# The last attention head of a fused attention and feed-forward kernel, worked through by token tiles in four passes

## What is computed

```python
x = L0_attn_x                                   # (2, 2048, 512) float32
x = x + attention(layernorm(x), Wq, Wk, Wv, memory, memory_norm, memory_weight)
x = x + ffn(layernorm(x), weight, weight_scale, input_scale)

# attention: 4 queries x 8 heads of 16 features; keys and values have 8 heads
scores = einsum('bsqhd,bthd->bqhst', qh, kh) * scale
a_dot  = einsum('bqhst,bthd->bsqhd', softmax(scores), vh)
a_mem  = sigma_q @ memory / (sigma_q @ memory_norm)          # sigma_q = elu(q)
out    = a_dot * (1 - w) + a_mem * w
# ffn
x_fp8 = clip(x / input_scale, -448, 448).astype(float8_e4m3fn)
y     = (x_fp8 * input_scale) @ (weight * weight_scale).T
```

## Time and profile before

| | |
|---|---|
| median of 3 runs | 2065.68 us (2064.96 to 2067.22) |
| the profiled execution's own time | 2065.7 us |
| its span in the profile | 2064.0 us |
| PE busy | 2029.0 us (98%), 27379 instructions |
| ACT busy | 1933.2 us (94%) |
| DVE busy | 1118.2 us (54%) |
| POOL busy | 82.3 us (4%) |
| first exponential of the heads starts | 211.6 us |
| last exponential of the heads starts | 2038.3 us |

### The profile page before, as it was taken

One profiled execution on the slowest core, in us unless ns is written; L12 is line 12 of the kernel. 1 busy time (PEld: TensorE's weight loads), 2 busy tenths in 40 slices (PEclk: granted clock), 3 DMA queues, 4 the chain that ended last, 5 costly groups with the idle time before them and its releaser, 6 DMA issues.

```text
span 2064.0 us, 62714 instructions
## 1 busy us (share of the span) xinstructions
PE 2029.0 (98%) x27379; PEld 897.5 (43%) x27380; DVE 1118.2 (54%) x1716; ACT 1933.2 (94%) x2180; POOL 82.3 (4%) x135
## 2 busy tenths in 40 slices
PE   8999999999999999999999999999999999999996
PEld 4555443334444444444444444444444444444442
DVE  5775544555445555455554555545555445555456
ACT  4555999999999999999999999999999999999995
POOL 3322000000000000000000000000000000000000
PEclk9999999999999999999999999999999999999998
DMA  5656211111111211112121111221121211121111
GB/s 191 196 186 206 62 48 35 36 48 51 51 42 39 72 50 51 40 44 61 50 51 50 53 49 51 51 65 36 45 49 51 71 37 43 51 71 51 33 43 42
DMA packets 137558, 131.57 MB, mean 64 GB/s; under 512 B 31520, under 2 KB 113824, under 8 KB 137312
## 3 DMA queue, kind: packets, MB, share of 16 engines
q1 hardware_dynamic: 135248, 125.11, 21.8%
q10 hardware_dynamic: 2064, 2.69, 0.4%
HBM read 86.57 MB, written 37.49 MB: 60 GB/s over the span
## 4 chain that ended last, share of the span: by engine, by line
PE 97%; DVE 2%; ACT 1%; DMA 0%; issue 0%; ACTq 0%; POOL 0%; DVEq 0%; POOLq 0%
PE ps L753 43%; PE ps L775 43%; PE ps L698 6%; PE ps L810 1%; PE ps L796 1%; PE ps L713 1%; PE ps L667 1%; DMA mem_aug<-in_memory_norm 0%; ACT pool L641 0%; DVE ps L1018 0%; DVE pool L906 0%; DVE parts L931 0%; DVE work L1177 0%; PE ps L682 0%; PE ps L675 0%
## 5 line engine op out<-in xcount | busy, mean ns | idle before, releaser
L641 ACT ACTIVATE pool<-ps 128x1024 f32<-128x1024 f32 x1984 | 1823.8, 1152 | 8.8 <-PE ps L753 5.7
L753 PE MATMUL ps<-q_st,k_st 99*32 99x512 bf16 x16384 | 1121.2, 379 | 3.2 <-issue 3.2
L775 PE MATMUL ps<-pool,v_st 128*32 128x512 f32 (+1 forms) x8704 | 1080.0, 567 | 0.5 <-ACT pool L641 0.5
L753 PEld LDWEIGHTS ps<-q_st,k_st 99*32 99x32 bf16 x16384 | 459.7, 96 | 815.7 <-issue 500.6
L775 PEld LDWEIGHTS ps<-pool,v_st 128*32 128x32 f32 x8704 | 281.5, 110 | 206.7 <-ACT pool L641 1.4
L1102 DVE STREAM_TRANSPOSE by_token<-ps 128x512 f32<-128x512 f32 x64 | 45.9, 717 | 484.0 <-PE ps L775 484.0
L1095 DVE SCALAR_TENSOR_TENSOR parts<-parts 128x1024 f32<-128x1024 f32 x192 | 235.3, 1225 | 6.6
L1081 DVE TENSOR_SCALAR parts<-ps 128x512 f32<-128x512 f32 x128 | 88.6, 692 | 131.4 <-PE ps L753 131.4
L698 PE MATMUL ps<-pool,wqT 128*128 128x512 f32 x256 | 111.4, 592 | 0.0
L596 ACT ACTIVATE parts<-ps 128x512 bf16<-128x512 f32 x40 | 23.9, 597 | 62.5 <-PE ps L698 62.5
L1154 DVE SCALAR_TENSOR_TENSOR y_out<-ps,scalars,resid 128x512 f32 x28 | 21.0, 752 | 113.2 <-PE ps L796 113.2
(11 more groups left out here) (125 smaller groups left out, 740.4 us busy)
## 6 DMA issues: line engine op xcount, KB each, us to landing
q_st<-q_aug SPq DMA_DIRECT2D x384, 64.0 KB
v_st<-v_aug SPq DMA_DIRECT2D x64, 256.0 KB
q_aug<-parts SPq DMA_DIRECT2D x96, 128.0 KB
k_st<-k_aug SPq DMA_DIRECT2D x64, 192.0 KB
sigma_kept<-y_out SPq DMA_DIRECT2D x32, 256.0 KB, 3.6
k_st<-k_aug SPq DMA_DIRECT2D x64, 128.0 KB
wqT<-sigma_kept SPq DMA_DIRECT2D x32, 256.0 KB, 3.3
resid<-in_x SPq DMA_DIRECT2D x7, 1024.0 KB, 9.1
```

Source lines behind the costliest of these rows:

```text
L641: act.activation(held[:, half_u * 2 * CH:half_u * 2 * CH + 2 * CH], sc[unit % SLOTS].rearrange("p a b -> p (a b)"), ACT.Exp, scale=EXP_UNIT)\
L753: last = pe.matmul(dst[VW * c:VW * c + VW, :], k_st[0:AUG, par, keys:keys + VW], q_st[0:AUG, par, q * CH:q * CH + CH], start=True, stop=True)
L775: last = pe.matmul(acc[par][VW * c:VW * c + VW, :].rearrange("v (i s) -> v i s", s=VW)[:, places, :], v_st[:, par, j, :], by_place[:, c, p ...
```

## The change

The last head is taken out of the loop over heads and worked through in four passes, one for each token tile. A pass has eight units (`TILE_UNITS`); a unit is now two key tiles x 4 queries x the 128 tokens of that tile, again 1024 columns. All 32 units of this head go to ACT; there is no late half and no `late_exps` on DVE. Products with the values follow three units behind (`last_weigh`), accumulate in `acc[1]` and `acc[0]` in turn, and have 128 columns in place of 512. After each pass DVE adds that tile's 128 tokens to the residual (`add_last_tile`), takes its statistics (`tile_moments`) and rounds it (`round_to_float8` into `xq[:, t]`). The last tile of chunk 6 gets its product at units 5 to 8 of this head, and its `ffn_out` stands ahead of the first pass's result. DVE's loop over chunks now ends at chunk 6, and chunk 7 is written out. At the end, the output of tile 0 is written between the statistics and the rounding of tile 3, and PE's order is turn 0, turn 1, product 0, turn 2, product 1, turn 3, product 2, product 3.

```diff
+LAST_HEAD = NG * HEADS - 1
+TILE_UNITS = ST // 2
+LAST_UNITS = TPC * TILE_UNITS
+LAST_RING = 2 * RING
+LAST_PRODUCT_AT = (5, 6, 7, 8)
...
         def _(act):
...
-            for n in range(NG * HEADS):
+            for n in range(LAST_HEAD):
...
+            for v in range(LAST_UNITS):
+                unit = LAST_HEAD * UNITS + v
+                act.wait_ge(scores_ready, unit + 1)
+                act.activation(last_probs[:, v % LAST_RING, :, :, :].rearrange("p x q s -> p (x q s)"),
+                               sc[unit % SLOTS].rearrange("p a b -> p (a b)"), ACT.Exp, scale=EXP_UNIT)\
+                    .then_inc(probs_ready, 1)
...
         def _(pe):
...
+            def last_scores(v):
+                unit = LAST_HEAD * UNITS + v
+                t, pair = divmod(v, TILE_UNITS)
+                by_tile = q_st[0:AUG, 1, :].rearrange("r (q t s) -> r t q s", q=QG, t=TPC)[:, t, :, :]
+                pe.wait_ge(probs_ready, unit - SLOTS + 1 + THREE_FREE)
+                for x in range(2):
+                    for c in range(P // VW):
+                        keys = (2 * pair + x) * P + c * VW
+                        last = pe.matmul(sc[unit % SLOTS][VW * c:VW * c + VW, x, :], k_st[0:AUG, 1, keys:keys + VW], by_tile,
+                                         start=True, stop=True)
+                last.then_inc(scores_ready, 1)
+
+            def last_weigh(v):
+                t, pair = divmod(v, TILE_UNITS)
+                by_place = last_probs[:, v % LAST_RING, :, :, :].rearrange("p x q (c s) -> p x c q s", c=P // VW)
...
+                for x in range(2):
+                    for c in range(P // VW):
+                        last = pe.matmul(acc[1 - t % 2][VW * c:VW * c + VW, 0:QG * VW].rearrange("v (q s) -> v q s", q=QG),
+                                         v_st[:, 1, 2 * pair + x, :], by_place[:, x, c, :, :],
+                                         start=(pair == 0 and x == 0), stop=(pair == TILE_UNITS - 1 and x == 1))
+                last.then_inc(pv_done, 1)
...
+            for v in range(LAST_UNITS):
+                last_scores(v)
+                if v + UNITS in WEIGH_AT:
+                    weigh_v(LAST_HEAD - 1, 0, WEIGH_AT[v + UNITS])
+                if v >= SLOTS:
+                    last_weigh(v - SLOTS)
+                if v in LAST_PRODUCT_AT:
+                    ffn_product((NG - 1) * TPC - 1, LAST_HEAD, LAST_PRODUCT_AT.index(v))
+            for v in range(LAST_UNITS - SLOTS, LAST_UNITS):
+                pe.wait_ge(probs_ready, LAST_HEAD * UNITS + v + 1 + THREE_FREE)
+                last_weigh(v)
...
-            for t in range(0, TPC, 2):
+            last_ffn_turn(0)
+            for t in range(1, TPC):
                 last_ffn_turn(t)
-                last_ffn_turn(t + 1)
-                last_ffn_product(t)
-                last_ffn_product(t + 1)
+                last_ffn_product(t - 1)
+            last_ffn_product(TPC - 1)
...
         def _(dve):
...
+            for t in range(TPC):
+                add_last_tile(t)
+                tile_moments(NT - TPC + t)
+                if t == TPC - 1:
+                    last_out(0)
+                round_to_float8(NT - TPC + t, xq[:, t, :], last_chunk=True)
+            for t in range(1, TPC):
+                last_out(t)
```

More of the change, by code:

```diff
@@ new lines, in _ @@
+            for n in range(LAST_HEAD):
+                head(n)
+            pe.wait_ge(operands_loaded[1], (LAST_HEAD // 2 + 1) * 16 * HEAD_LOADS)
+            for v in range(LAST_UNITS):
[6 more added lines that the diff above has]
+                    ffn_product((NG - 1) * TPC - 1, LAST_HEAD, LAST_PRODUCT_AT.index(v))
@@ L1111, in add_head, with add_last_tile, tile_moments, round_to_float8 @@
                 dve.tensor_tensor(cols, cols, head_out[:, :, :, :], ALU.add)
-            def chunk_moments(g):
+            def add_last_tile(t):
+                n = LAST_HEAD + t
+                dve.wait_ge(pv_done, LAST_HEAD * ST + (t + 1) * TILE_UNITS)
+                tile = last_by_token[:, t, :, :]
+                dve.transpose(tile.rearrange("p q v -> p (q v)"), acc[1 - t % 2][:, 0:QG * VW]).then_inc(acc_read, 1)
+                dve.wait_ge(acc_read, n + 1 + TWO_FREE)
+                dve.reciprocal(rden[:, :, t], tile[:, :, DH]).then_inc(rden_ready, 1)
+                dve.wait_ge(rden_ready, n + 1)
+                dve.tensor_tensor(head_out[:, :, t, :], tile[:, :, 0:DH],
+                                  rden[:, :, t].unsqueeze(2).to_broadcast([P, QG, DH]), ALU.mult).then_inc(head_out_ready, 1)
+                dve.wait_ge(head_out_ready, n + 1)
+                cols = resid[:, NT - TPC + t, :].rearrange("p (q f) -> p q f", q=QG)[:, :, KV - DH:KV]
+                dve.tensor_tensor(cols, cols, head_out[:, :, t, :], ALU.add)
+            def tile_moments(i):
                 dve.drain()
-                for t in range(TPC):
-                    dve.bn_stats(stats[:, t, :], resid[:, bass.ds(g * TPC + t, 1), :].rearrange("p a d -> p (a d)"))
+                dve.bn_stats(stats[:, 0, :], resid[:, bass.ds(i, 1), :].rearrange("p a d -> p (a d)"))
                 dve.drain()
[L1118 to L1126, removed]
+                dve.bn_aggr(moments[:, 0, 0, :], stats[:, 0, :]).then_inc(f_moments, 1)
+            def round_to_float8(i, rounded, last_chunk=False):
                 row = resid[:, bass.ds(i, 1), :].rearrange("p a d -> p (a d)")
                 xs, big = work[:, 0, :], work[:, 4, :]
[L1129 to L1132, removed]
                 dve.wait_ge(f_rstd, i + 1)
@@ L1156, in ffn_out @@
                                          ALU.mult, ALU.add).then_inc(y_ready, 1)
[L1158 to L1180, removed]
             def add_memory(g, q, half_q):
@@ L1206, in _, with first_of_pair, second_of_pair, last_out @@
                 add_head(2 * hp + 1, 1, 0, 2 * hp + 1)
[L1207 to L1220 removed]
+            def first_of_pair(g, hp):
+                late_exps(g * HEADS + 2 * hp, 0)
+                add_memory(g, hp, 0)
+                tile_moments((g - 1) * TPC + hp)
+                round_to_float8((g - 1) * TPC + hp, xq_now[:, :])
+                add_memory(g, hp, 1)
+                add_head(g * HEADS + 2 * hp, 0, g, 2 * hp)
+            def second_of_pair(g, hp):
+                late_exps(g * HEADS + 2 * hp + 1, 1)
+                ffn_out(g - 1, hp)
+                add_head(g * HEADS + 2 * hp + 1, 1, g, 2 * hp + 1)
+            with dve.Fori(1, NG - 1) as g:
+                with dve.Fori(0, HEADS // 2) as hp:
+                    first_of_pair(g, hp)
+                    second_of_pair(g, hp)
+            for hp in range(HEADS // 2 - 1):
+                first_of_pair(NG - 1, hp)
+                second_of_pair(NG - 1, hp)
+            first_of_pair(NG - 1, HEADS // 2 - 1)
+            ffn_out(NG - 2, TPC - 1)
+            def last_out(t):
                 dve.wait_ge(ffn_ready, (NG - 1) * TPC + t + 1)
```

48 lines of the change are left out of this document (20 added, 28 removed).

## The result

| | before | changed |
|---|---|---|
| median of 6 runs | 2065.78 us (2064.96 to 2067.22) | 2057.41 us (2056.45 to 2058.46) |
| ratio to before | | 0.9956, 95% interval 0.9946 to 0.9966 |
| profiled execution, its span | 2065.7, 2064.0 us | 2056.68, 2055.0 us |

The change makes the kernel 8.4 us faster, 0.4%; the forecast was 2057.2 us. The span of the profiled execution is 9.0 us shorter.

What follows compares the result with a forecast made beforehand. PE and ACT bound the body side by side; DVE almost alone orders the tail, its piece 17.56 us. Terms 0.7 + 0.0 - 10.65 + 1.45 = -8.5 gave span 2055.5, time 2057.2 us, range 2054.8 to 2060.5.

Steps and rivals of the forecast that it cites:

- end of the last exponential: Last head on ACT: 32 exponentials instead of 31, ending at 2040.1 instead of 2039.4, +0.7 us.
- from there to the last tile on DVE: Last exponential to DVE's last tile: 1.2 us as before, the tile starting 0.5 us late behind tile 2; 0.0 us.
- DVE on the last tile: DVE's tail: 6.9 us for one tile instead of 17.56, last rounding ends at 2048.2; -10.65 us.
- from the last rounding to the end: Kernel's end: turn, two products, output and store take 7.3 us at the low clock, 5.86 before; +1.45 us.
- The price of the value group: Last head on PE: a unit's values in 128 columns take 0.44 us, from `memory_products`, where 0.43 stood.
- mild feeding loss: Last head on PE, rival: 0.56 us a value group makes PE the bound; +2.9 us, 2060.1; 9%.
- PE be the slower engine for nine units only: Last head: PE takes 9.1 us against ACT's 8.1 for nine units, then waits for ACT; ACT loses some 0.4.
- PE never waits for ACT: Sign of failure in the passes: if it happened, the forecast was wrong through feeding.
- my two cases: PE clock, last products: low, 7.3 us after the last rounding; or high, 5.6 us and 2055.5, a rival at 30%.
- The small matmuls cannot be fed: Last head on PE, rival: each of 16 costs its own 0.108 us; +37 us, 2094.6; 5%.
- DVE becomes the bound: DVE in the passes, rival: a tile costs 7.7 us and no longer fits in 7.2; +3.1, 2060.3; 7%.
- the late wait: Passes, rival: late DMA transposes at unit 5 or a late accumulator read costs as much as is won, 2065; 3%.

Runs made afterwards that it cites:

- b2: Changed kernel with one more 128x512 DVE instruction, its result unused, in the rounding of tiles 0, 1 and 2 of the last chunk: 2057.61 us, ratio 0.9959.
- a4: Changed kernel with statistics and rounding of all four tiles moved behind the last pass, PE's tail in pairs as before: 2065.57 us, ratio 0.9995.
- a1: Changed kernel plus 15 idle PE matmuls of 512 columns between the product of tile 1 and the turn of tile 3: 2055.26 us, ratio 0.9947.
- b1: Changed kernel with the last head's value matmuls halved to 64 columns, 32 loads and 32 matmuls per unit instead of 16: 2065.04 us, ratio 0.9994.
- e1: b1 with the score matmuls also halved, to 256 columns, 48 loads and 48 matmuls per unit instead of 40 and 40: 2070.94 us, ratio 1.0021.
- a3: Changed kernel with product 2 ahead of turn 3 and 11 idle PE matmuls behind product 2: 2054.65 us, ratio 0.9945.
- c2: a3 together with the 12 idle matmuls of c1: 2053.89 us, ratio 0.9937.
- c1: Changed kernel plus 12 idle PE matmuls of 512 columns before head 0, tail left alone: 2054.67 us, ratio 0.9941.

## Why the prediction was right

Sign and mechanism came as forecast, and the time within 0.5 us of span. That the median, 2057.41 us, lies only 0.2 from the forecast is in part luck: the six runs fall into two groups (2056.45 to 2056.79 and 2058.04 to 2058.46), the median lies between them, and the errors of the four terms have both signs. By the four terms, in the profiled executions:

| term | forecast | measured |
|---|---|---|
| end of the last exponential | +0.7 | +1.25 (2039.4 to 2040.65) |
| from there to the last tile on DVE | 0.0 | -0.4 (0.76 us instead of 1.2) |
| DVE on the last tile | -10.65 | -10.9 (6.62 us: 2041.41 to 2048.03) |
| from the last rounding to the end | +1.45 | +1.1 (6.97 us) |
| sum | -8.5 | -9.0 |

*Body.* The price of the value group, 0.44 us from the memory products, was exact, and with it fell the rule of the Trainium skill ("TensorE: Matmul & The Clock Gate", Back-to-back issue gap), 81 ns a pair, for this shape: 512 matmul instructions with 32-column weights, on four column groups, ran here at 0.028 us each. The mild feeding loss did not come either. One step failed: I let PE be the slower engine for nine units only and then wait for ACT. PE went from unit to unit in 0.87 us to the end of the scores (the last ones start at 2037.98), without a wait; with a margin of 0.03 to 0.05 us per unit it needs the rest of the head to take back what the first nine units cost. ACT kept its own pace behind them all the same. From the first start to the last it took 28.44 us (2010.91 to 2039.35), which is the forecast's 31 x 0.904 + 0.4; it lost the 0.4 where the product of chunk 6 lengthens PE's units (starts at 2016.33, 2017.28, 2018.37 and 2019.45). The product's inputs were not late. What I had sized wrong is the length of the last exponential, from ACT's timeline:

```profile
2039.35 1.30 ACT L651 ACTIVATE pool<-ps 128x1024 f32<-128x1024 f32 x1
```

I had taken 1.05 us from the earlier trace rows. While nothing holds ACT its rows start 0.904 us apart, but each is some 0.013 us longer than the one before, so that they end 0.917 apart, and what depends on them follows the ends: the last two value groups start at 2039.78 and 2040.70. That is 0.25 of the 0.55 us by which the term was too small. The other 0.3 came from before the head, where the first exponential was 0.28 us later. So my sign of failure, "PE never waits for ACT", was badly put: up to the last scores it happened, and was harmless.

*Is DVE free?* A tile cost 6.62 us, not 6.9: the head's result for 128 tokens took 1.13 us (2020.79 to 2021.92), I had 1.3, and the rest 5.50 for 5.64. So the last tile started 0.06 us behind its sums and not 0.5. That DVE and the sums would meet was right, and b2 shows how near: some 0.35 us of slack a pass.

*DVE's piece.* Right to 0.3 us, and a4 shows that nearly the whole gain is there.

*Tail.* The low clock came after 3.6 us without work, and a1 shows cause and price (1.55 us of the 1.7 between my two cases). It fell 0.2 us into product 2, so the turn ran at the high level: from the last rounding to the first product it took 0.29 us (I had 0.5), and the products 3.44 (3.62), which is the 0.35 us that the term was too large.

*Rivals.* "The small matmuls cannot be fed" did not happen at 128 columns, but its direction is real: b1 loses all of the gain at 64 columns, through a limit that I had not thought of, the delivery of instructions, and e1 is slower than before. The upper pace of loads that I worked from, 16 in 0.56 us, was misread: it counts the length of the last load, and the starts are 0.030 us apart, 0.48 us for a group. "DVE becomes the bound" and the late wait did not happen.

## What to carry to other kernels

Where work waits at the very end because a sum is finished for all tiles at once, turn the loops of the last round: finish the sum tile by tile, and only one tile's chain stays behind it. Price the finer instructions from the nearest group of the same shape in the trace, and compare the follower's time per tile with the length of a pass: here 6.6 us against 7.0. When the tail has become short, look at what its idle times do to the clock: a few idle matmuls gave 1.6 us more, a fifth of the change's whole gain. And before splitting matmuls further, count PE's instructions per us: 52 went through here without a stop, 70 did not.

## What the runs showed of the hardware

- PE took 70 to 73 instructions per us over tens of us (loads and matmuls counted) and no more: after every 256 instructions it stood still, for 0.4 to 1.8 us, with "issue" as the only reason, until 1.2 to 1.6 us after a 16 KB packet of the instruction queue had landed (b1, e1). The Trainium skill, "Runtime: NRT & Kernel Launch", Instruction fetch mechanics, says that instructions are streamed in 16 KiB blocks at a cost that is mostly hidden. The 16 KB packets are here; the cost is hidden at 52 instructions per us, and not when PE is given 80 for each 0.9 us of ACT's work.
- 32-column float32 weight loads on four column groups went 0.030 us apart, on average over a group, beside matmuls of 128 columns and 0.022 apart beside matmuls of 64: the pace in the earlier trace rows was no limit of the loads.
- ACT's exponentials of 128 x 1024, with nothing to wait for, started 0.904 us apart and ended 0.917 apart; the recorded length of one grew from 1.02 to 1.30 us over 22 of them (2020.37 to 2039.35).
- Ahead of the low clock PE had no work for 3.6 us; the clock fell after the work had begun again (2048.5), and stayed until 2051.9. With that gap filled (a1, a3, c2) it did not fall. In c1, with the same 3.6 us (2044.57 to 2048.18), it fell 1.2 us before the work began again, so the moment is not fixed to PE's next work:

```profile
2044.00:2048.00 4.00, 0.57 (x3) 0.08 (x1) 3.58 (x8) 0.34 (x1) 0.46 (x1) 0.87 0.17 66
```
